# A causal Toeplitz convolution in the last layer: full 384 x 384 products cut into 128-blocks with summed taps and block differences

## The reference, cut to what matters

```
U_plus  = causal_conv(phi[:, k], u)                 # for every filter k
U_minus = sgn * causal_conv(phi[:, k], sgn * u)     # sgn = +1, -1, +1, ...
out = einsum('btkd,k,kde->bte', U_plus, sigma**0.25, Mpp)
    + einsum('btkd,k,kde->bte', U_minus, sigma**0.25, Mpm) + (3 short taps with M_u)
x = x + sum over m of weight[m] * out_m             # m: first 1, 1/2, 1/4, 1/8 of the tokens
```

## Time and profile before

| | |
|---|---|
| median of 3 runs | 8442.53 us |
| profiled execution | 8448.98 us, its span 8447.1 us |
| PE busy | 7665.0 us (91% of the span) |
| weight loads busy | 5961.6 us |
| DVE busy | 5345.4 us |
| ACT busy | 3817.7 us |
| the convolution block's line 2265, matmuls | 11520 |

### The profile page before, as it was taken

How to read it: one execution, slowest core, us unless ns; L and a number is a source line. 1 busy time by engine, 2 the same in 40 slices (tenths; PEclk the granted TensorE clock), 3 DMA queues, 4 the chain that set the end, 5 groups by cost and what they waited for, 6 DMA issues and landing times. The chain is left out here.

```text
span 8447.1 us, 141745 instructions
## 1 busy us (share of the span) xinstructions
PE 7665.0 (91%) x51342; PEld 5961.6 (71%) x51342; DVE 5345.4 (63%) x8084; ACT 3817.7 (45%) x8029; POOL 3663.7 (43%) x2420
## 2 busy tenths in 40 slices
PE   8999899997999979999467788699799999999999
PEld 6888678885888858887356677356666666666666
DVE  7999799996999969999445555455532222222222
ACT  5887578873888748876112222244421111111111
POOL 5888468882888828886355554110000000000000
PEclk9999999998999989999689899899999999999999
DMA  2333123331333313332565554000022222222222
GB/s 64 90 91 89 59 75 90 91 88 45 91 90 90 89 44 91 91 90 73 160 181 159 157 156 135 6 3 0 7 89 86 87 91 87 80 94 92 80 86 77
DMA packets 459084, 727.20 MB, mean 86 GB/s; under 512 B 51687, under 2 KB 364040, under 8 KB 456497
## 3 DMA queue, kind: packets, MB, share of 16 engines
q1 hardware_dynamic: 406705, 550.52, 21.1%
q0 software_dynamic: 51840, 169.91, 7.0%
HBM read 686.77 MB, written 33.46 MB: 85 GB/s over the span
## 5 line engine op out<-in xcount | busy, mean ns | idle before, releaser
L591 POOL TENSOR_TENSOR l_arena<-l_arena 128x768 f32<-128x768 f32 x1536 | 2778.7, 1824 | 472.0 <-DVE l_arena L541 411.2
L541 DVE TENSOR_TENSOR_SCAN l_arena<-l_arena,psum 128x384 f32<-128x384 f32 x3072 | 2866.4, 983 | 78.2 <-PE psum L382 42.8
L475 ACT ACTIVATE l_arena<-l_arena,l_A 128x384 f32<-128x384 f32 x3072 | 1665.3, 604 | 81.4 <-DVE l_arena L541 81.3
L384 PE MATMUL psum<-l_arena 128*128 128x128 f32 x11520 | 1581.2, 285 | 28.7 <-DVE l_arena L541 26.2
L384 PEld LDWEIGHTS psum<-l_arena 128*128 128x128 f32 x11520 | 1407.5, 192 | 184.9 <-issue 114.4
L2344 DVE TENSOR_TENSOR st_Uc<-psum,st_both 128x384 f32<-128x384 f32 x512 | 285.5, 558 | 1701.0 <-PE psum L2265 1701.0
L395 PE MATMUL psum<-l_ident,l_arena 128*128 128x128 f32 x9216 | 1260.2, 273 | 53.0 <-ACT l_yT L481 45.5
L395 PEld LDWEIGHTS psum<-l_ident,l_arena 128*128 128x128 f32 x9216 | 1053.7, 141 | 64.3 <-POOL l_arena L591 41.5
L2265 PE MATMUL psum<-st_F,st_xt 128*128 128x384 f16 (+2 forms) x6912 | 1002.1, 290 | 0.0
L2265 PEld LDWEIGHTS psum<-st_F,st_xt 128*128 128x128 f16 x6912 | 649.5, 97 | 385.3 <-issue 62.3
L1148 POOL DMA_INDIRECT l_G<-neighbours,l_idx x648 | 618.6, 955 | 665.4 <-PE psum L1196 325.0
(11 more groups left out here) (397 smaller groups left out, 7668.8 us busy)
## 6 DMA issues: line engine op xcount, KB each, us to landing
l_arena<-c_rows SPq DMA_DIRECT2D x1536, 192.0 KB, 3.0
st_FS<-filter_sums SPq DMA_DIRECT2D x128, 641.0 KB, 7.6
st_F<-filter_parts SPq DMA_DIRECT2D x128, 576.5 KB, 6.4
neighbours<-l_xt SPq DMA_DIRECT2D x256, 72.0 KB
st_mab<-in_st_mp SPq DMA_DIRECT2D x68, 256.0 KB, 7.6
st_mab<-in_st_mm SPq DMA_DIRECT2D x68, 256.0 KB, 7.9
l_G<-neighbours,l_idx POOLq DMA_INDIRECT x648
l_gnx<-in_x SPq DMA_DIRECT2D x4, 1152.0 KB, 5.9
```

Of the source, the lines that this page charges most:

```text
L384: mm = pe.matmul(ps[:, o:o + P], dtuT[:, g % 2, t, h * P:(h + 1) * P], diagB[:, rank[s] % 3, t, :], start=True, stop=True)
L475: act.activation(decay[:, s % NDC, h, :], dtv[:, g % 2, h, :], ACT.Exp, scale=A[:, g // NRC, h, n:n + 1]).then_inc(s_exp, 1)
L541: dve.tensor_tensor_scan(hbuf[:, n, h, flip], decay[:, s % NDC, h, flip], ps[:, BANK * (2 * (s % 2) + h):BANK * (2 * (s % 2) + h) + RC][:, ...
L591: pool.tensor_tensor(hC[:, s % NHC], hbuf[:, s % NS], Cs[:, s % NCS, :].unsqueeze(1).broadcast_to([P, 2, RC]), ALU.mult).then_inc(s_hc, 1)
```

## The change

A full 384 x 384 Toeplitz product has nine 128 x 128 blocks, of which five are different. The change makes each such product from six 128-block products. Three ("own", `own(...)`) multiply each input block with the sum of three neighbouring blocks of taps. Three ("pairs", `pairs(...)`) multiply differences of two input blocks with a single block of taps. The pair results are added to one output block and subtracted from another. The triangles stay as they are. So a full product is 18 matmuls of 128 columns instead of 9 of 384 columns.

What goes with it:

- PSUM: the totals are packed in banks 0 to 4, `OWN`, `PAIR` and `LOW` (triangles) are banks 5, 6 and 7. Zeroing is five matmuls, and the last third's totals are in three pieces of 128.
- DVE: eight operations in a unit instead of two (lines 2428 to 2442). ACT: four copies in a unit instead of two.
- PE order: the next unit's shared part and first triangle are issued before mix(u, 2), over the ends of filters and of turns too. The last turn of the loop is written out a second time, and the last unit has nothing to carry.
- Head block: ACT copies into `xp` in three pieces, DVE sorts in six operations of 384, POOL makes the differences of halves and of blocks (ten operations), and PE transposes 42 blocks in 14 groups, each with one ACT and one DVE operation of 384.
- Setup: five sets of summed taps instead of two. `F` rows get shorter (641 instead of 1153 taps), `FS` has 5 sets of 385 instead of 2 sets of 641.

```diff
-                        for u in range(2 * NU):
...
-                            conv(u, "shared")
-                            if u:
-                                pe.wait_ge(s_ed, (unit + u) * 2)
-                                mix(u - 1, 2)
-                            conv(u, "first")
-                            pe.wait_ge(s_ea, (unit + u) * 2 + 1)
-                            conv(u, "second")
...
+                    def own(u, at, three, x0, start):
+
+                        r, z, q, shift = shape(u)
+                        for i in range(LB):
+                            for m, (xpart, fpart) in enumerate(PARTS):
+                                mm = pe.matmul(ps[:, at + i * P:at + (i + 1) * P], xt[:, xpart, x0 + LB - 1 - i, :],
+                                               FS[:, r, fpart, z, three, shift + i * P:shift + (i + 1) * P],
+                                               start=(start and i + m == 0), stop=(i == LB - 1 and m == 2), skip_group_check=True)
+                        return mm
+
+                    def pairs(u, tap, group, start):
+
+                        r, z, q, shift = shape(u)
+                        for e, d in enumerate((0, 2, 1)):
+                            for m, (xpart, fpart) in enumerate(PARTS):
+                                mm = pe.matmul(ps[:, PAIR + e * P:PAIR + (e + 1) * P], xt[:, xpart, PAIR0 + (3 * q + group) * 3 + e, :],
+                                               tap[:, r, fpart, z, shift + d * P:shift + (d + 1) * P],
+                                               start=(start and e + m == 0), stop=(e == 2 and m == 2), skip_group_check=True)
+                        return mm
...
+                            pe.wait_ge(s_ea, copied + 2)
+                            own(u, OWN, 3, q * HB + LB, False)
+                            pairs(u, FS[:, :, :, :, 0], 1, False).then_inc(s_cv, 1)
...
+                            mix(u, 0)
+                            triangle(u, q * HB + 2 * LB)
+                            own(u, LOW, 4, q * HB, False).then_inc(s_cv, 1)
+                            pe.wait_ge(s_ea, copied + 4)
+                            pairs(u, FS[:, :, :, :, 1], 0, True).then_inc(s_cv, 1)
+                            pe.wait_ge(s_ed, done + 3)
+                            mix(u, 1)
...
+                                shared(v)
+                                pe.wait_ge(s_ed, done + 5)
+                                shared_pairs(v)
+                                first(v)
+                            pe.wait_ge(s_ed, done + 8)
+                            mm = mix(u, 2)
...
-                                dve.tensor_tensor(Uc[:, c, :], ps[:, bank * BANK:bank * BANK + RC], both[:, u % 2, :],
-                                                  ALU.add if c == 1 else ALU.subtract).then_inc(s_ed, 1)
...
+                            dve.tensor_tensor(second, ps[:, OWN:OWN + RC], pair_1[:], ALU.add).then_inc(s_ed, 1)
+                            dve.wait_ge(s_ed, at + 1)
+                            dve.tensor_tensor(second[:, P:], second[:, P:], pair_1[:, 0:2 * P], ALU.subtract).then_inc(s_ed, 1)
+                            dve.tensor_tensor(second[:, 0:P], second[:, 0:P], pair_1[:, 2 * P:], ALU.subtract).then_inc(s_ed, 1)
...
+                            dve.tensor_tensor(third, ps[:, LOW:LOW + RC], own_s[:, u % 2, :], ALU.subtract).then_inc(s_ed, 1)
...
+                            dve.tensor_tensor(pair_2[:], ps[:, PAIR:PAIR + RC], pair_s[:, u % 2, :], ALU.subtract).then_inc(s_ed, 1)
```

More of the change, by code:

```diff
@@ L2198, in layer3_spectral @@
             with nc.Block() as block:
-                NU, KINDS = 4, ("shared", "first", "second", "third")
-                NG = NU * len(KINDS)
+                NU = 4
+                OWN, PAIR, LOW = (BANK * i for i in (5, 6, 7))
                 USES = (KF // 2 + 1, KF // 2)
@@ new lines, in _, with shape, triangle @@
+                    PARTS = ((0, 0), (0, 1), (1, 0))
+                    def shape(u):
+                        r, z, q = u // NU, u // 2 % 2, u % 2
+                        return r, z, q, (0 if (z and q) else 1)
+                    def triangle(u, x0):
+                        r, z, q, shift = shape(u)
+                        for j in range(LB):
+                            for m, (xpart, fpart) in enumerate(PARTS):
+                                mm = pe.matmul(ps[:, LOW + j * P:LOW + RC], xt[:, xpart, x0 + j, :], F[:, r, fpart, z, shift:shift + RC - j * P],
+                                               start=(j + m == 0), stop=(j == LB - 1 and m == 2), skip_group_check=True)
+                        return mm
@@ new lines, in mix, with shared @@
+                    def mix(u, c):
+                        r, z, q, _ = shape(u)
+                        for m, lo, hi, o in totals(z ^ q, c):
+                            mm = pe.matmul(ps[:, o:o + hi - lo], Wm[:, r, z, m, :], Uc[:, c, lo - c * RC:hi - c * RC],
+                                           start=False, stop=False, skip_group_check=True)
+                        return mm
+                    def shared(u):
+                        own(u, OWN, 2, 2 * HB + u % 2 * LB, True)
+                        return None
@@ L2304, in _ @@
+                    with pe.Fori(0, KF // 2 - 1) as i:
+                        filters_pair(i, False)
+                    filters_pair(KF // 2 - 1, True)
                 @block.vector
@@ L2376, in sum_tiles @@
 def sum_tiles(parts):
-    whole = [bass.AP(parts.tensor, part * KF * 2 * 2 * SR, [[4 * SR, KF], [1, P], [SR, 4], [1, SW]]) for part in range(2)]
+    row = SETS * SETW
+    whole = [bass.AP(parts.tensor, part * KF * 2 * row, [[2 * row, KF], [1, P], [SETW, 2 * SETS], [1, SW]]) for part in range(2)]
     return lambda part, k: whole[part][ds(k, 1)].rearrange("o p z x -> p (o z) x")
```

281 lines of the change are left out of this document (161 added, 120 removed).

## The result

The changed kernel takes 8176.42 us in the median of four runs (8169.36 to 8179.0), the kernel before 8438.72 in four beside them (8424.89 to 8447.69). The ratio is 0.9688, with a 95% interval of 0.9673 to 0.9703. The profiled execution took 8177.77 us. The forecast was 8184.

The account below looks back on a forecast made before the run. PE, busy in all 540.9 us of a batch's convolution at peak column pace, was taken as the bound; 8449.0 - 287 + 14 + 6 + 2 = 8184 us, own range 8150 to 8225, with 8140 to 8310 holding about 0.83.

Parts of the forecast that it names:

- The price of a short matmul: PE's 54 matmuls of 128 columns in a unit: 0.056 us each with overlapped weight loads, 3.02 us against 4.40 before.
- load-bound rival: PE's 54 short matmuls in a unit bound by weight loads: slower from 75 ns each, 8723 us at 95 ns; chance 0.11.
- The unit: PE's work for one convolution unit: 7.24 us without waits, 7.31 with the mean stall, where it was 8.45.
- The stall in a filter's first unit: PE waits for DVE's `pair_2` at the next shared pairs, one unit in four: 0.3 us, 0.07 in the mean.
- The cover of mix 2: Next unit's shared part and first triangle ahead of mix 2 hide DVE's chain: ready at 6.5 us, wanted at 6.8.
- another rival: DVE's chain of eight dependent operations late in every unit: some 0.4 us in the mean, + 100 us, 8285; chance 0.13.
- The head block: Start of each batch: POOL's ten differences take 9 us, block 13.3 instead of 9.7, 3.6 us more, 14 in four.
- Instructions don't stay in the engine: PE's loop or batch code outgrows the engine and is fetched at 28 jumps back: + 45 us, 8230; chance 0.05.
- nothing waits for them: DMA of `F` and `FS` for a filter, some 7 us with 25 us available: no wait, even if twice as slow.
- Setup: Setup block: DVE's set sums of taps, with low halves, casts and four sums of three, add 6 us, once.
- batch ends: End of each batch: the last unit has nothing between mix 1 and DVE's chain, so PE waits 1.2 us.
- -287 + 14 + 6 + 2: Whole kernel: convolution loop gain 287 us; added head blocks 14, setup 6, short taps' pieces and residual additions 2.

Follow-up runs that it names:

- run 1: Changed kernel with the nine short matmuls of the shared own product issued twice in each unit; 8318.95 us, ratio 0.982 to the kernel before.
- run 2: Changed kernel with own and pair matmuls of 64 columns instead of 128 (result not the reference's); 7658.12 us, ratio 0.9366 to the kernel before.
- Run 3: Changed kernel with nine 384-column matmuls replacing own and pair products, new order kept (result not the reference's); 8502.69 us, ratio 1.0042 to the kernel before.
- run 4: Changed kernel with mix 2 directly behind mix 1, not carried over the next unit's shared product and first triangle; 8738.34 us, ratio 1.0316 to the kernel before.
- run 5: Like run 4, with DVE's matrix step behind the third's operations instead of ahead of them; 8305.12 us, ratio 1.016 to the kernel before.
- run 7: Changed kernel with mix 2 not carried over turn ends and no second copy of the last turn; 8251.52 us, ratio 0.9743 to the kernel before.
- run 8: Changed kernel without POOL's eight block differences, PE transposing other blocks instead (result not the reference's); ratio 0.9668 to the kernel before, same as the changed kernel's.
- run 9: Kernel before with only PE's last turn of the loop written out a second time; 8181.32 us, ratio 1.0005 to the kernel before.
- run 6: Changed kernel with both matrix steps at the end of DVE's unit, measured twice: 7892.81 us (ratio 0.9654 to the kernel before) and 8156.35 us (0.9664).

## Why the prediction was right

- **The price of a short matmul** (the decisive term, 0.056 us from three matmuls in a row): right, 56 ns in the median, 57 in eighteen in a row (run 1). The load-bound rival falls; run 2 shows why, since the same loads follow at 29 to 31 ns where there are only 64 columns. Run 3 shows that the columns are the whole gain. The sustained 81 ns that the Trainium skill, "TensorE: Matmul & The Clock Gate", section "Back-to-back issue gap", states for 128 columns do not hold in this stream.
- **The unit:** 7.24 us predicted without waits, 7.21 measured. The stall in a filter's first unit 0.3 predicted, 0.25 measured, once in a filter and nowhere else. With the predicted mean of 7.31 the 63 units would gain 531.2 - 460.5 = 70.7 us, 283 in four batches; with the measured 7.26 they gain 295.2.
- **The cover of mix 2:** right that it hides DVE's chain, whose lateness was another rival. Runs 4 and 5 give the worth of having any cover: 1.64 us a unit, about 420 us in all, more than the gain; so the short products need it. The kernel before had a part of it already, and what the new place adds to that wasn't run (90 us by the estimate in run 5). The carry over turns' ends alone is worth 46 us (run 7).
- **The head block:** 3.6 us more were predicted, with POOL's ten differences as the cause. In the first batch that is right: +2.7 us, PE waits for POOL, and without eight of the differences the block is 2.2 us shorter (run 8). POOL's ten take 8.2 us there, the price by width; I had taken 9. In the other three batches it is wrong: +4.6 to 4.8 us, and nobody waits for POOL. There PE starts late, behind the fetch of its code (run 9 shows that cause in the kernel before, 3.8 us of the start), and behind it come 14 pairs of ACT and DVE evictions of 0.5 us (7.33 us against 4.83). These blocks are about 2 us longer than the first. That the term came out near is luck: a wait was left out, and it took the place of the one that was priced.
- **Instructions don't stay in the engine**, a rival with 0.05 and + 45 us: half true. The turn stays, as the earlier trace rows said; no packet moves in the middle of a batch. The batch of some 3,100 loads and matmuls does not. The Trainium skill, "Runtime: NRT & Kernel Launch", section "Instruction fetch mechanics", has room for 2048 instructions, which I quoted without taking a price for it. The limit can't be told exactly here: a batch with some 1,700 loads and matmuls and some 80 other recorded instructions was fetched again (run 7), and run 1's turn of some 1,550 was kept.
- **DMA, "nothing waits for them":** missed at the start of a batch. In the profile above the shared product of the second batch waits 2.3 us for `FS`; in the profile of the changed kernel taken in run 6 it waits in all four batches, 5.0 us together. The loads of `FS` now take 8.8 us in the median, where they took 6.7 in the stretch of the earlier trace rows and 7.6 over all batches from 6300 us on. In the middle of a batch nothing waits, as said.
- **Setup** +6.7, with the normalization behind it (predicted 6), **batch ends** 1.2 us each on PE (predicted 1.2): right.

By its own terms: -287 + 14 + 6 + 2 = -265 predicted. The measured terms begin and end at other places, since one unit of each batch lies outside the marks: -295.2 in the 63 units, +17.0 between the batches, +3.6 from the first head block to the first mark, +6.7 setup, +1.1 tail, and -4.4 of scatter ahead of it all, together -271.2. Divided like this the forecast was -283 for the loop and +18 for the rest; -295.2 and +28.4 are measured. That the total came within 6 us is in part luck: the two errors and the scatter go against each other.

## What to carry to other kernels

Where PE has no idle time and its timeline shows columns at full pace, count columns: in f16 more and shorter matmuls had no price for their loads at 128 columns, and at 64 each took half of that time. But the products that save columns add a chain on DVE, and it has to be laid under other PE work from the start; here running without that cover costs more than the columns save. A piece of DVE work that nobody waits for soon belongs behind the one that PE waits for. A loop's body written out twice costs code, and its fetch can show as a first instruction that comes late with the releaser "issue" or with an operation that was long done. Writing it once does not help if the rest is still too long (run 7).

The sums of taps and the differences of blocks are larger than what they are made of. So the changed kernel also halves the scale of the tokens ahead of their split into two f16 parts (`XS` is 2^10 instead of 2^11) and doubles the scale of the mixing. No run shows what happens without it.

## What the runs showed of the hardware that was not expected

- A matmul of 64 columns in f16 with its own 128 x 128 load goes every 29 to 31 ns, though a load is recorded at 97 ns in the mean.
- Behind 54 of 64 waits of PE of 1.85 us, one in four units, the clock fell to half (nine short matmuls in 0.96 us, mean granted clock 0.96 in the batch, run 4). Behind waits of 1.50 us (run 4) and 1.20 us (runs 4 and 5) it never did.
- A recorded wait of 1.20 us behind matmuls costs 1.37 us (run 5).
- Where the code of the next batch had to be fetched, PE's first instruction came some 3.8 us late (5.5 us after the block's start instead of 1.7, run 9). It happened with some 1,700 loads and matmuls in a batch (run 7) and not with some 1,100 (before); a turn of some 1,550 stayed (run 1).
